# Four engine lists in a new order, and the query variance in one step per column block

## The chip, the cores and the metric

One core of one Trainium2 chip runs the whole model. The metric is the device time of one execution in microseconds; three runs of the kernel before gave 465.56, 465.67 and 467.3 us, median 465.67. Lower is better.

## What is computed

x is four sequences of 256 tokens, 128 wide. Two layers are applied, each an attention over a context and a feed-forward part, both behind a tanh gate; every part takes the layer norm of x.

```python
x = x + tanh(g_xattn[0]) * autocorrelation_attention(ln(x), ctx)   # FFTs over the sequence, top 5 delays
x = x + tanh(g_ffn[0])   * product_key_experts(ln(x))
x = x + tanh(g_xattn[1]) * rotary_attention(ln(x), ctx)            # 16 heads of 8
x = x + tanh(g_ffn[1])   * routed_experts(ln(x))                   # 8 experts, 336 wide
# product_key_experts, its head:
q = x @ w_q                                       # 128 -> 2048
q = (q - mean(q)) * rsqrt(var(q) + 1e-5) * bn_gamma + bn_beta     # over all 1024 tokens
sim = q . keys                                    # 2 x 8 heads x 32 keys
sx, sy = top_k(sim[0], 8), top_k(sim[1], 8)       # then top 8 of the 64 sums: 64 experts a token
h = softmax(scores) * gelu(x . down_embed[i]);  out = sum(h * up_embed[i])
# routed_experts: for each expert e
out += score[e] * (silu(x @ gate_w[e].T) * (x @ up_w[e].T)) @ down_w[e].T
```

## The kernel before

The program is written for each engine by hand: TensorE (PE in the profile), VectorE (DVE), ScalarE (ACT), GpSimd (POOL) and SyncE (SP), with semaphores between them. Each engine takes its instructions strictly in the order in which they are written, so an instruction that waits holds all that stand behind it. The first 90 us (the first attention, the layer norm of all 1024 tokens, the head of the product-key part) have an order fixed in the code. From there on the work is cut into named steps, and the string ORDER (line 60) lists for each engine which step comes next; the function `steps` reads it. A word is the step's name, a digit for the sequence b (0 to 3), a point and a number k: `token1.4` is step `token`, sequence 1, piece 4; `norms10.0` is `norms1`, sequence 0; `turn_32.0` is `turn_3`, sequence 2.

The query variance (lines 898 to 905). The variance of each of the 2048 query columns comes from the covariance of the normed x, cov (128x128). TensorE forms cov times w_q for 16 blocks of 128 columns, three blocks to a PSUM bank (six banks, the last with one block). VectorE copies the means, multiplies the bank by w_qT (L904), waits for that, and sums each block (L905). From the 16 x 128 variances come scaled keys keyS (L914) and, with 16 small matmuls, the matrix M; ScalarE copies M, and then `similar` t multiplies the tokens of tile t by M. `down_all` n forms one half of x times the embedding table (PE), which `gelu` n takes (ACT). EARLY says how many of them stand ahead of M's matmuls: with EARLY = 4, three on TensorE's list, n = 0 to 2, and three gelus on ScalarE's.

The steps that this text speaks of, in the order in which one sequence passes them:

- `best`, `where`, `pair` (DVE: L929, L936, L942 to L945), with `cands`, `gap`, `look_a` (POOL): the top 8 of each group and of the sums. `weight` (DVE, L978 to L992) turns them into expert numbers and weights; it waits for `look_a`, `gap` (POOL) and `soft` (ACT). `number` (POOL) splits the expert numbers and waits for both `weight` steps of its sequence. `onehots` (PE, then ACT) transposes them, `groups` (DVE, L1009 to L1027) makes the one-hot Y.
- `place` (DVE, L1035) makes a one-hot X for 16 tokens, `token` (PE, ps<-Y,Xb) multiplies it by Y, `half` (ACT, L611) copies, `weigh` (DVE, L1047 and L1052) forms HD. `mix` (PE, 16 matmuls of ps<-sb_upl,HDb) gives the part's output.
- `norms1` (DVE L1060 to L1068, then POOL L439 to L446, then ACT L627) adds it to x and normalises; `turn_2`, `query` (PE), `rope` (DVE L786 to L791), `turn_q` (PE, then ACT), four `by_query` (PE, ps<-KTb,Sb) and `max` (DVE L1097), `neg_max`, four `score` (PE, ps<-Sb,KTb), `prob` (ACT L651), `value` (PE, ps<-probs,V), `keep` (ACT), `out_turn`, `attend`, `project`: the second attention.
- `norms3` (DVE, POOL, ACT), `turn_3` (PE L1515), `route1` and `route2` (PE, ACT, DVE), `rank` (DVE); 21 `gate` (PE, ps<-...,sb_guT, into two banks by turns), 21 `silu` (ACT L694), 21 `times` (POOL L433 for sequences 0 and 1, DVE L1167 for 2 and 3), 8 `down` (PE, ps<-dnb,Sb) and `gather` (DVE L1155, L1157), `moe_out`. `addb` (POOL L459) adds a bias to x.

TensorE's bank 2 and bank 3 are each used by many steps in turn; `claim` makes each wait until the one before has been taken out, so a `down` waits for the `gather` of the last `down` or the `keep` of the last `value`. On ScalarE, `table` (L564) loads the function table where exp, gelu and silu follow each other.

The lines of VectorE that the second part of the change touches:

```python
v.tensor_copy(var[:, 2, c0:c0 + m], cw[:, :, D])
link(v.tensor_tensor(w, cw[:, :, 0:D], ld["w_qT"][:, c0:c0 + m, :], ALU.mult))
i = v.tensor_reduce(var[:, 3, c0:c0 + m], w, AX, ALU.add)
i.then_inc(sem("cw_used"), 1)
```

## Time and profile before

| what | value |
|---|---|
| median of three runs | 465.67 us |
| the profiled execution, own time | 464.96 us |
| its span, first to last instruction | 462.8 us |
| TensorE / VectorE / ScalarE / GpSimd busy | 381.2 / 331.8 / 193.8 / 108.9 us |
| mean granted clock of TensorE | 0.856 |

Busy time is a share of the whole span and mixes stages with different limits. TensorE's records overlap the pipeline, so its busy time is no measure of its peak; idle time ahead of a row, in square brackets, names who released it. The granted clock is given in tenths of full speed: 5 is 1.2 GHz, 10 (printed 9 or 1.00) is 2.4 GHz.

### The profile page before, as it was taken

The page shows a single profiled execution, that of the slowest core. Times are in us where ns is not written, and L with a number is a line of the kernel's source. Part 1 is how long each engine was busy: PE and PEld are TensorE (multiplying, and loading weights), DVE is VectorE, ACT ScalarE, POOL GpSimd, SP SyncE. Part 2 cuts the span into 40 slices and gives each one's busy share as a digit, 9 for nine tenths or more (in the row PEclk, how much of TensorE's full clock was granted, in tenths as well). Part 3 has the DMA queues.
Part 4 walks back from the last instruction along what each step waited for, and adds up shares of the span by engine and source line. Part 5 has one row for each costly group of instructions (what it writes and reads, how often), then busy time and mean ns, then how long its engine had stood idle before and what let it go on. Part 6 is the DMA issues. An engine that isn't in the chain of part 4 may idle for free.

```text
span 462.8 us, 7976 instructions
## 1 busy us (share of the span) xinstructions
PE 381.2 (82%) x2812; PEld 293.8 (63%) x2812; DVE 331.8 (72%) x1235; ACT 193.8 (42%) x393; POOL 108.9 (24%) x221
## 2 busy tenths in 40 slices
...
DVE  6996575999999999999998385866416543344533
...
PEclk9989897985565555766589999999999999999999
...
GB/s 220 336 220 0 1 1 2 1 157 2 1 1 0 2 0 1 1 1 1 1 0 2 1 2 1 1 3 12 1 1 1 0 13 2 1 0 1 11 1 11
DMA packets 5773, 11.80 MB, mean 25 GB/s; under 512 B 2021, under 2 KB 4326, under 8 KB 5223
## 3 DMA queue, kind: packets, MB, share of 16 engines
...
q14 instruction: 17, 0.13, 0.1%
...
## 4 chain that ended last, share of the span: by engine, by line
PE 39%; DVE 9%; ACT 3%; issue 3%; POOL 1%; POOLq 0%; DVEq 0%; ACTq 0%
PE ps L1193 37%; DVE Y L1027 2%; DVE Xb L1035 1%; PE ps L1435 1%; DVE mx L1097 1%; ACT L564 1%; ACT Sb L694 1%; DVE sb_downT L1017 1%; DVE Sb L1167 1%; DVE xnb L1157 0%; DVE HDb L1052 0%; ACT probs L651 0%; POOL rs L441 0%; ACT xnb L627 0%; PE ps L1515 0%
## 5 line engine op out<-in xcount | busy, mean ns | idle before, releaser
L1193 PE MATMUL ps<-dnb,Sb 128*128 128x128 f32 x448 | 57.1, 279 | 3.9 <-DVE xnb L1157 1.5
L1193 PEld LDWEIGHTS ps<-dnb,Sb 128*128 128x128 f32 x448 | 53.2, 192 | 9.8 <-issue 7.1
L1193 PE MATMUL ps<-Y,Xb 128*128 128x32 f16 x512 | 39.9, 250 | 18.8 <-DVE Xb L1035 13.2
L1193 PEld LDWEIGHTS ps<-Y,Xb 128*128 128x128 f16 x512 | 36.9, 164 | 27.3 <-DVE Xb L1035 18.3
L694 ACT ACTIVATE Sb<-ps 128x256 f32<-128x256 f32 x84 | 31.3, 380 | 41.5 <-PE ps L1193 41.4
L471 ACT ACTIVATE Sb<-ps 128x256 f32<-128x256 f32 (+2 forms) x54 | 26.6, 494 | 43.7 <-PE ps L1193 32.3
L1193 PE MATMUL ps<-ctxTb,sb_guT 128*128 128x256 f32 x168 | 44.0, 396 | 0.8 <-DVE Sb L1167 0.7
L1035 DVE TENSOR_TENSOR Xb<-sb_downT,iox 128x2048 f16<-128x2048 f16 x32 | 40.4, 1274 | 4.6 <-PE ps L1193 4.4
L1193 PE MATMUL ps<-Xb,sb_guT 128*128 128x256 f32 x168 | 43.1, 398 | 0.3
L1097 DVE TENSOR_REDUCE mx<-ps 128x8 f32<-128x2048 f32 x16 | 36.6, 2289 | 5.0 <-PE ps L1193 4.7
L1157 DVE SCALAR_TENSOR_TENSOR xnb<-ps,score,xnb 128x128 f32<-128x128 f32 x56 | 17.0, 345 | 31.4 <-PE ps L1193 31.3
L564 ACT ACT_TABLE_LOAD x29 | 37.2, 1283 | 0.5
L651 ACT ACTIVATE probs<-ps 128x1024 f32<-128x1024 f32 x32 | 31.4, 1018 | 10.9 <-PE ps L1193 10.8
L1193 PEld LDWEIGHTS ps<-Xb,sb_guT 128*128 128x128 f32 x168 | 30.9, 197 | 7.1 <-DVE Sb L1167 1.7
L1167 DVE TENSOR_TENSOR Sb<-Sb,ps 128x256 f32<-128x256 f32 x42 | 17.1, 419 | 25.0 <-ACT Sb L694 24.9
L1193 PEld LDWEIGHTS ps<-ctxTb,sb_guT 128*128 128x128 f32 x168 | 30.1, 194 | 7.8 <-DVE Sb L1167 2.1
L433 POOL TENSOR_TENSOR Sb<-Sb 128x256 f32<-128x256 f32 x28 | 24.3, 879 | 33.6 <-ACT Sb L694 33.4
L1193 PE MATMUL ps<-KTb,Sb 32*128 32x256 f32 x256 | 24.0, 501 | 9.1 <-DVE mx L1097 4.9
L1193 PE MATMUL ps<-sb_upl,HDb 128*128 128x128 f32 x128 | 20.2, 332 | 5.4 <-DVE HDb L1052 5.4
L1193 PEld LDWEIGHTS ps<-sb_upl,HDb 128*128 128x128 f32 x128 | 19.5, 244 | 7.3 <-DVE HDb L1052 7.3
L1193 PEld LDWEIGHTS ps<-KTb,Sb 32*128 32x128 f32 x256 | 14.5, 235 | 14.7 <-DVE mx L1097 6.3
L382 POOL TENSOR_SCALAR tixf<-tix 128x64 f32<-128x64 uint32 x8 | 4.0, 503 | 80.3 <-DVE tix L936 80.3
...
## 6 DMA issues: line engine op xcount, KB each, us to landing
...
```

The source lines that it names most:

```text
L433: g.tensor_tensor(av[:, m % 6, :], av[:, m % 6, :], up[m % 3], ALU.mult).then_inc(sem("av_ready"), 1)
L471: act.activation(dst, src, ACT.Copy, scale=scale).then_inc(sem(s), 1)
L564: act.activation(sm[:, 63:64], tg[:, 0:1], func).then_inc(sem("table_ready"), 1)
L651: act.activation(probs[:, g % 2, 2 * half:2 * half + 2, :], ps[:, 4 + 2 * half:6 + 2 * half, :], ACT.Exp, scale=float(1.0 / np.sqrt(DK))). ...
L694: act.activation(av[:, m % 6, :], ps[:, m % 2, 0:256], ACT.Silu).then_inc(sem("gate_ready"), 1)
L1017: link(v.tensor_tensor(elS[:, :, :], elT[:, 0, :].unsqueeze(1).broadcast_to([P, EH, P]), ld["io16"][:, :].unsqueeze(2).broadcast_to([P, EH ...
L1027: i = v.tensor_tensor(Y[r, q, k, :, :], Yq[r, :, :], whl[r, k, :].unsqueeze(1).broadcast_to([64, EH, P]), ALU.mult)
L1035: v.tensor_tensor(X[:, c % 2, :, :].rearrange("p (c e) t -> p c e t", c=EH), elS[:, :, c * TC:c * TC + TC].unsqueeze(2).broadcast_to([P, E ...
L1097: v.tensor_reduce(mx[:, :, 4 * g:4 * g + 4].rearrange("p t r -> p r t"), ps[:, 4:8, :].rearrange("p r (t k) -> p r t k", t=2), AX, ALU.max)\
L1157: i = v.scalar_tensor_tensor(macc[:, t, :], y, w, macc[:, t, :], ALU.mult, ALU.add)
L1167: v.tensor_tensor(av[:, m % 6, :], av[:, m % 6, :], ps[:, m % 2, 256:512], ALU.mult).then_inc(sem("av_ready"), 1)
L1193: return pe.matmul(o, l, r, start=start, stop=stop)
```

## The change

First, ORDER is replaced: each engine's list holds the same steps as before (244 for TensorE, 210 for ScalarE, 217 for VectorE, 76 for GpSimd), in another order. Second, the variance: instead of one multiply and one sum for a bank of three blocks, with a wait between them, there is one `scalar_tensor_tensor` for each block, which multiplies twice (once by 1.0) and gives the sum of its products in an accumulated output. Third, EARLY goes from 4 to 2: one `down_all` and one `gelu` stand ahead of M, the others of the first four behind the first four `similar`. The diff, the lists cut to the lines that the text speaks of:

```diff
     "pe": """
-onehots0.0 token0.0 token0.1 token0.2 token0.3 token0.4 token0.5 token0.6 token0.7 mix0.0 turn_20.0 query0.0 turn_q0.0
-onehots1.0 by_query0.0 by_query0.1 token1.0 by_query0.2 token1.1 by_query0.3 token1.2 neg_max0.0 token1.3 score0.0
-token1.4 score0.1 value0.0 token1.5 score0.2 token1.6 value0.1 score0.3 token1.7 value0.2 mix1.0 value0.3 onehots2.0
-out_turn0.0 turn_21.0 query1.0 attend0.0 project0.0 turn_q1.0 token2.0 by_query1.0 turn_30.0 token2.1 gate0.0
...
-gate0.6 route20.0 neg_max1.0 token2.5 score1.0 token2.6 gate0.7 score1.1 value1.0 token2.7 score1.2 value1.1 mix2.0
-score1.3 value1.2 onehots3.0 down0.0 down0.1 gate0.8 gate0.9 turn_22.0 gate0.10 query2.0 gate0.11 gate0.12 value1.3
-turn_q2.0 down0.2 by_query2.0 gate0.13 out_turn1.0 gate0.14 by_query2.1 down0.3 token3.0 attend1.0 by_query2.2
...
-score3.0 down1.7 gate2.2 route22.0 score3.1 gate2.3 value3.0 value3.1 score3.2 down2.0 gate2.4 gate2.5 score3.3
-value3.2 gate2.6 gate2.7 down2.1 gate2.8 down2.2 gate2.9 value3.3 gate2.10 out_turn3.0 gate2.11 gate2.12 down2.3
-gate2.13 attend3.0 gate2.14 project3.0 gate2.15 gate2.16 down2.4 gate2.17 down2.5 gate2.18 gate2.19 turn_33.0 gate2.20
-down2.6 gate3.0 gate3.1 route13.0 gate3.2 route23.0 down2.7 gate3.3 gate3.4 gate3.5 down3.0 gate3.6 gate3.7 down3.1
...
+onehots0.0 token0.0 token0.1 token0.2 token0.3 token0.4 token0.5 token0.6 token0.7 mix0.0 onehots1.0 turn_20.0
+query0.0 turn_q0.0 token1.0 token1.1 by_query0.0 token1.2 token1.3 by_query0.1 token1.4 by_query0.2 token1.5
+by_query0.3 token1.6 neg_max0.0 token1.7 score0.0 mix1.0 score0.1 value0.0 onehots2.0 score0.2 value0.1 score0.3
+value0.2 turn_21.0 value0.3 query1.0 out_turn0.0 turn_q1.0 attend0.0 project0.0 by_query1.0 token2.0 turn_30.0
+token2.1 gate0.0 by_query1.1 gate0.1 token2.2 gate0.2 by_query1.2 gate0.3 token2.3 gate0.4 by_query1.3 route10.0
+token2.4 gate0.5 neg_max1.0 route20.0 token2.5 score1.0 gate0.6 gate0.7 token2.6 value1.0 score1.1 down0.0 token2.7
+score1.2 value1.1 mix2.0 down0.1 gate0.8 onehots3.0 gate0.9 value1.2 gate0.10 down0.2 gate0.11 score1.3 turn_22.0
+gate0.12 query2.0 down0.3 token3.0 turn_q2.0 value1.3 token3.1 by_query2.0 gate0.13 out_turn1.0 gate0.14 by_query2.1
...
+project2.0 score3.0 gate1.16 down1.4 gate1.17 down1.5 gate1.18 turn_32.0 gate1.19 gate1.20 route12.0 gate2.0 score3.1
+down1.6 gate2.1 route22.0 score3.2 value3.0 gate2.2 down1.7 gate2.3 value3.1 score3.3 value3.2 down2.0 gate2.4
+value3.3 gate2.5 out_turn3.0 gate2.6 gate2.7 down2.1 gate2.8 attend3.0 gate2.9 project3.0 gate2.10 gate2.11 down2.2
+gate2.12 down2.3 gate2.13 gate2.14 turn_33.0 gate2.15 down2.4 gate2.16 down2.5 gate2.17 gate2.18 route13.0 gate2.19
+route23.0 gate2.20 down2.6 gate3.0 gate3.1 down2.7 gate3.2 gate3.3 gate3.4 gate3.5 down3.0 gate3.6 down3.1 gate3.7
...
     "act": """
...
-keep0.0 half1.5 soft2.1 prob0.4 prob0.5 keep0.1 half1.6 prob0.6 prob0.7 half1.7 keep0.2 keep0.3 onehots2.0 norms1_b1.0
-soft3.0 soft3.1 turn_21.0 attend0.0 turn_q1.0 half2.0 norms3_b0.0 turn_30.0 half2.1 silu0.0 half2.2 silu0.1 silu0.2
-silu0.3 half2.3 silu0.4 half2.4 route10.0 silu0.5 neg_max1.0 half2.5 prob1.0 half2.6 prob1.1 route20.0 prob1.2 prob1.3
-half2.7 keep1.0 prob1.4 prob1.5 keep1.1 prob1.6 keep1.2 prob1.7 onehots3.0 norms1_b2.0 silu0.6 silu0.7 silu0.8 silu0.9
...
-turn_33.0 silu2.20 silu3.0 route13.0 silu3.1 silu3.2 route23.0 silu3.3 silu3.4 silu3.5 silu3.6 silu3.7 silu3.8 silu3.9
...
+turn_20.0 soft2.0 half1.0 turn_q0.0 half1.1 half1.2 half1.3 half1.4 half1.5 soft2.1 half1.6 neg_max0.0 half1.7 prob0.0
+prob0.1 prob0.2 prob0.3 onehots2.0 keep0.0 prob0.4 prob0.5 soft3.0 norms1_b1.0 keep0.1 prob0.6 prob0.7 keep0.2
+turn_21.0 keep0.3 attend0.0 turn_q1.0 half2.0 norms3_b0.0 turn_30.0 half2.1 silu0.0 silu0.1 half2.2 silu0.2 silu0.3
+half2.3 silu0.4 route10.0 half2.4 silu0.5 neg_max1.0 route20.0 half2.5 prob1.0 prob1.1 keep1.0 half2.6 prob1.2 soft3.1
+prob1.3 half2.7 prob1.4 silu0.6 keep1.1 silu0.7 prob1.5 silu0.8 onehots3.0 norms1_b2.0 keep1.2 silu0.9 silu0.10
+silu0.11 turn_22.0 prob1.6 prob1.7 half3.0 turn_q2.0 keep1.3 silu0.12 silu0.13 half3.1 silu0.14 silu0.15 half3.2
...
+silu2.9 silu2.10 silu2.11 norms3_b3.0 silu2.12 silu2.13 turn_33.0 silu2.14 silu2.15 silu2.16 silu2.17 silu2.18
+route13.0 silu2.19 silu2.20 route23.0 silu3.0 silu3.1 silu3.2 silu3.3 silu3.4 silu3.5 silu3.6 silu3.7 silu3.8 silu3.9
...
     "dve": """
...
-weigh0.2 weigh0.3 place0.5 weigh0.4 place0.6 weigh0.5 place0.7 weigh0.6 where1.0 weigh0.7 pair1.0 where1.1 weight1.0
-norms10.0 best2.0 pair1.1 where2.0 weight1.1 rope0.0 best2.1 pair2.0 groups1.0 max0.0 place1.0 place1.1 max0.1
-weigh1.0 place1.2 max0.2 weigh1.1 place1.3 max0.3 neg_max0.0 weigh1.2 place1.4 weight2.0 weigh1.3 place1.5 where2.1
-weigh1.4 pair2.1 place1.6 weigh1.5 place1.7 weight2.1 weigh1.6 best3.0 best3.1 weigh1.7 where3.0 where3.1 pair3.0
-norms11.0 pair3.1 groups2.0 place2.0 attend0.0 place2.1 weight3.0 rope1.0 norms30.0 weight3.1 weigh2.0 max1.0 weigh2.1
-place2.2 place2.3 max1.1 weigh2.2 place2.4 max1.2 weigh2.3 place2.5 weigh2.4 max1.3 neg_max1.0 route20.0 place2.6
-weigh2.5 place2.7 weigh2.6 rank0.0 weigh2.7 norms12.0 gather0.0 groups3.0 place3.0 place3.1 gather0.1 rope2.0
...
+weight1.0 norms10.0 weight1.1 best2.0 where2.0 groups1.0 best2.1 place1.0 pair2.0 rope0.0 place1.1 weight2.0 weigh1.0
+place1.2 place1.3 weigh1.1 where2.1 weigh1.2 max0.0 place1.4 place1.5 weigh1.3 max0.1 weigh1.4 pair2.1 max0.2 place1.6
+weigh1.5 max0.3 weigh1.6 neg_max0.0 place1.7 weight2.1 weigh1.7 best3.0 where3.0 best3.1 pair3.0 norms11.0 where3.1
+groups2.0 weight3.0 rope1.0 attend0.0 place2.0 place2.1 norms30.0 pair3.1 weigh2.0 max1.0 weigh2.1 place2.2 place2.3
+max1.1 weigh2.2 place2.4 max1.2 weigh2.3 max1.3 neg_max1.0 weigh2.4 place2.5 route20.0 place2.6 weigh2.5 rank0.0
+place2.7 weigh2.6 gather0.0 weigh2.7 weight3.1 norms12.0 gather0.1 groups3.0 place3.0 gather0.2 rope2.0 gather0.3
...
     "pool": """
-look_a0.1 cands1.0 cands1.1 look_a1.0 gap1.0 look_a1.1 norms10.0 cands2.0 gap1.1 look_a2.0 number1.0 cands2.1 gap2.0
-addb0.0 look_a2.1 gap2.1 number2.0 cands3.0 cands3.1 look_a3.0 look_a3.1 norms11.0 gap3.0 addb1.0 gap3.1 norms30.0
-number3.0 times0.0 times0.1 times0.2 times0.3 times0.4 times0.5 norms12.0 addb2.0 times0.6 times0.7 times0.8 times0.9
...
+look_a0.1 cands1.0 gap1.0 cands1.1 look_a1.0 gap1.1 look_a1.1 norms10.0 number1.0 cands2.0 look_a2.0 cands2.1 gap2.0
+gap2.1 look_a2.1 cands3.0 look_a3.0 number2.0 addb0.0 norms11.0 gap3.0 look_a3.1 cands3.1 norms30.0 gap3.1 times0.0
+times0.1 times0.2 times0.3 times0.4 times0.5 number3.0 times0.6 norms12.0 times0.7 times0.8 times0.9 times0.10
...
         G_BANK = [4 + n % 4 for n in range(2 * EH)]
-        EARLY = 4
+        EARLY = 2
         WARM = 3
         DIRECT = (2, 3)
...
             copy(M[:, :], ps[:, 7, :], "M_ready")
             similar(2)
             similar(3)
-            gelu(EARLY - 1)
-            for n in range(EARLY, EH):
+            for n in range(EARLY - 1, 4):
+                gelu(n)
+            for n in range(4, EH):
                 similar(n)
                 gelu(n)
             soft(0, 0)
...
                 cw = ps[:, bank, 0:m * (D + 1)].rearrange("p (c d) -> p c d", d=D + 1)
                 w = tmp[:, c0 * D:(c0 + m) * D].rearrange("p (c d) -> p c d", d=D)
                 v.tensor_copy(var[:, 2, c0:c0 + m], cw[:, :, D])
-                link(v.tensor_tensor(w, cw[:, :, 0:D], ld["w_qT"][:, c0:c0 + m, :], ALU.mult))
-                i = v.tensor_reduce(var[:, 3, c0:c0 + m], w, AX, ALU.add)
+                for c in range(m):
+                    i = v.scalar_tensor_tensor(w[:, c, :], cw[:, c, 0:D], 1.0, ld["w_qT"][:, c0 + c, :], ALU.mult, ALU.mult,
+                                               accum_out=var[:, 3, c0 + c:c0 + c + 1])
                 i.then_inc(sem("cw_used"), 1)
             v.wait_ge(sem("cw_used"), len(CW_BANK))
             link(v.tensor_tensor(var[:, 2, :], var[:, 2, :], var[:, 2, :], ALU.mult))
...
             for t in range(4):
                 shifted(t)
             pe.wait_ge(sem("xn1T_ready"), 1)
-            for n in range(3):
+            for n in range(EARLY - 1):
                 down_all(n)
             for c in range(16):
                 if c % 8 == 0:
...
             pe.wait_ge(sem("xcT_ready"), 1)
             for t in range(4):
                 similar(t)
-            down_all(3)
+            for n in range(EARLY - 1, 4):
+                down_all(n)
             for t in range(4, NT):
                 shifted(t)
                 similar(t)
```

## Rows read from the trace of the kernel before

**Rows 1.** Page, part 2: VectorE busy tenths and granted clock in 40 slices of the span.

```profile
DVE  6996575999999999999998385866416543344533
...
PEclk9989897985565555766589999999999999999999
```

**Rows 2.** Windows: stretch in us, then busy us (instructions) per engine, PEclk, DMA.

```profile
80.00:220.00 140.00, 84.99 (x614) 59.68 (x612) 136.26 (x695) 36.23 (x72) 47.55 (x112) 0.64 0.04 14
...
247.00:283.00 36.00, 32.27 (x321) 25.01 (x320) 23.68 (x53) 21.77 (x45) 9.97 (x16) 1.00 0.00 1
...
366.00:392.00 26.00, 24.48 (x213) 17.94 (x212) 8.67 (x34) 22.18 (x41) 3.29 (x6) 1.00 0.02 7
...
420.00:432.00 12.00, 10.35 (x51) 7.93 (x50) 6.76 (x27) 8.49 (x16) 0.00 (x0) 0.86 0.01 1
```

**Rows 3.** Timeline of PE, 57 to 73 us: start, duration, operation [idle before, releaser].

```profile
57.54 3.74 PE L1193 MATMUL ps<-Gb,simb 128*128 128x129 f32 x32
...
64.55 2.74 PE L1193 MATMUL ps<-dnb,sb_downT 128*128 128x512 f32 x6
...
67.27 3.76 PE L1193 MATMUL ps<-Gb,simb 128*128 128x32 f32 x32
```

**Rows 4.** Timeline of DVE, 52 to 65 us.

```profile
52.70 1.37 DVE L894 TENSOR_SCALAR xnb<-sb_x,mv,rs 128x128 f32<-128x128 f32 x5
...
58.48 0.16 DVE L903 COPY var<-ps 128x3 f32<-128x3 f32 x1 [4.42 <-PE ps L1193]
...
58.56 0.55 DVE L904 TENSOR_TENSOR Gb<-ps,simb 128x384 f32<-128x384 f32 x1
...
59.61 0.15 DVE L903 COPY var<-ps 128x3 f32<-128x3 f32 x1
...
64.79 0.17 DVE L908 TENSOR_TENSOR var<-var 128x16 f32<-128x16 f32 x1
```

**Rows 5.** Timeline of DVE, 99 to 264 us.

```profile
99.23 3.06 DVE L929 MAX8 top<-simb 128x8 f32<-128x32 f32 x32
...
221.22 0.40 DVE L786 TENSOR_TENSOR Sb<-ps,cs 128x256 f32<-128x256 f32 x1
...
223.63 0.83 DVE L978 TENSOR_TENSOR hot<-pkf,iox 128x1280 f16<-128x1280 f16 x1
...
227.52 0.41 DVE L1047 TENSOR_TENSOR Xb<-Xb,ps 128x256 f32<-128x256 f32 x1
...
263.00 0.48 DVE L1060 SCALAR_TENSOR_TENSOR sb_x<-ps,tg,sb_x 128x256 f32<-128x256 f32 x1 [4.27 <-PE ps L1193]
```

**Rows 6.** Timeline of POOL, 207 to 215 us.

```profile
207.15 0.22 POOL L439 TENSOR_SCALAR rs<-mv 128x2 f32<-128x2 f32 x1 [1.50 <-DVE mv L1068]
...
211.79 0.62 POOL L446 TENSOR_TENSOR nb<-rs 128x2 f32<-128x2 f32 x1
...
213.47 1.01 POOL L459 TENSOR_TENSOR sb_x<-sb_x,sb_bo 128x256 f32<-128x256 f32 x1
```

**Rows 7.** Timeline of PE, 198 to 283 us.

```profile
198.82 1.43 PE L1193 MATMUL ps<-sb_upl,HDb 128*128 128x128 f32 x5 [1.47 <-DVE HDb L1052]
...
216.43 0.77 PE L1193 MATMUL ps<-sb_Wq,ctxTb 128*128 128x128 f32 x2 [2.36 <-ACT ctxTb L471]
...
225.63 2.09 PE L1193 MATMUL ps<-KTb,Sb 32*128 32x256 f32 x16
...
228.75 0.69 PE L1515 MATMUL ps<-sb_ident,xnb 128*128 128x128 f32 x2 [1.04 <-ACT xnb L627]
...
238.30 1.15 PE L1193 MATMUL ps<-KTb,Sb 32*128 32x256 f32 x16
```

**Rows 8.** Timeline of PE, 425 to 431 us.

```profile
425.98 4.43 PE L1193 MATMUL ps<-Xb,sb_guT 128*128 128x256 f32 x12
```

**Rows 9.** Page, part 5: groups of ScalarE: busy us, mean ns; idle before.

```profile
L564 ACT ACT_TABLE_LOAD x29 | 37.2, 1283 | 0.5
...
L651 ACT ACTIVATE probs<-ps 128x1024 f32<-128x1024 f32 x32 | 31.4, 1018 | 10.9 <-PE ps L1193 10.8
```

More of the change, by code:

```diff
@@ L82 @@
+gate2.12 down2.3 gate2.13 gate2.14 turn_33.0 gate2.15 down2.4 gate2.16 down2.5 gate2.17 gate2.18 route13.0 gate2.19
+route23.0 gate2.20 down2.6 gate3.0 gate3.1 down2.7 gate3.2 gate3.3 gate3.4 gate3.5 down3.0 gate3.6 down3.1 gate3.7
+gate3.8 gate3.9 gate3.10 down3.2 gate3.11 down3.3 gate3.12 gate3.13 gate3.14 gate3.15 down3.4 gate3.16 gate3.17
+gate3.18 gate3.19 down3.5 gate3.20 down3.6 down3.7
 """,
     "act": """
-onehots0.0 half0.0 half0.1 half0.2 half0.3 half0.4 half0.5 half0.6 half0.7 soft1.0 norms1_b0.0 turn_20.0 soft1.1
@@ L95 @@
[L95 to L98 removed]
+onehots0.0 half0.0 half0.1 half0.2 half0.3 half0.4 half0.5 half0.6 half0.7 soft1.0 soft1.1 onehots1.0 norms1_b0.0
@@ L112 @@
-weigh3.5 moe_out0.0 weigh3.6 weigh3.7 rank1.0 norms13.0 gather1.0 gather1.1 rope3.0 gather1.2 gather1.3 max3.0
-attend2.0 max3.1 gather1.4 max3.2 norms32.0 max3.3 gather1.5 neg_max3.0 gather1.6 times2.0 times2.1 gather1.7
-moe_out1.0 route22.0 rank2.0 times2.2 times2.3 gather2.0 times2.4 times2.5 times2.6 times2.7 gather2.1 gather2.2
-times2.8 times2.9 times2.10 attend3.0 times2.11 times2.12 gather2.3 times2.13 times2.14 norms33.0 times2.15 gather2.4
-times2.16 times2.17 gather2.5 times2.18 times2.19 times2.20 gather2.6 times3.0 route23.0 times3.1 times3.2 rank3.0
```

55 lines of the change are left out of this document (27 added, 28 removed).

## The prediction

> **What bounds the kernel now.** I read the busy slices first, then busy time by windows, then each engine's timeline, laid step by step against ORDER (the number of instructions of each step is known from the code, so every row has its step). Two stages follow each other. From 80 to 220 us VectorE is busy 136.3 of 140 us, while TensorE has 85 busy us and, mostly, half the clock [rows 1, 2]; its list sets the pace. From the start of `turn_30.0` at 228.75 [rows 7] the gates exist, and TensorE has work to the end: between 247 and 283 us it idles 3.7 us, between 366 and 392 1.5, between 420 and 432 1.65 [rows 2]. What TensorE has to do from `turn_30.0` on is, but for the order, the same set of steps in both lists. So the time is the start of `turn_30.0`, plus that work, plus the waits and half-clock stretches in it. An order that only shuffles the second stage can win those waits and no more.
>
> **The head: variance and EARLY.** The block runs on VectorE from 58.48 to 64.79, 6.3 us, 1.13 a bank of three blocks [rows 4]. The new form has six copies, 0.08 each to the next instruction, and 16 products of 128x128; five plain 128x128 instructions take 1.37, so 0.27 each [rows 4]: 0.5 + 4.3 = 4.8 us, 1.5 less. No row shows an accumulated output. It costs nothing at the least; at the most I take another small instruction, 0.08 as the copy has, which is 16 x 0.08 = 1.3 us and leaves a gain of 0.2. I take the middle, **-0.9 us**, range 0.2 to 1.5. In VectorE's page of the Trainium skill ("VectorE: DVE Perf Modes", section "Two Vector instructions with no wait between them") such an operation counts as two instructions, the main one and an accumulator read; no run here shows it yet. By that rule the gain would be 0.2, without it 1.5.
> TensorE must be there as soon: M's matmuls start at 67.27, straight behind three `down_all` (64.55, 2.74 for three) [rows 3]. With EARLY = 4 no gain on VectorE could pass; with 2 it is free at 64.55 + 0.91 = 65.5, room for 1.8. The two products and gelus that are moved stand behind the first four `similar`, ahead of tiles that VectorE needs much later. They cost nothing while ScalarE's `soft` 0 comes in time for `weight0.0`; if not, the 0.9 is lost there.
>
> **VectorE up to `weigh1.7`.** In the old order the last piece of sequence 1 is weighed just ahead of 198.82, where `mix1.0` starts [rows 7]. The new list has the same steps ahead of it but `best3.0` and `best3.1`, 2 x 1.53 [rows 5]: -3.0 us. New waits are possible in two places. `onehots1.0` stands ahead of `turn_20.0` on both TensorE and ScalarE and waits for `number1.0`, which waits for `weight1.1`: `groups1.0` may come 0.6 late. And `weight2.0` stands close behind `gap2.0`: 0.3. The four `max0` now alternate with `place` and `weigh`, each long enough to cover a half-clock `by_query` of 2.1. Sum **-2.1**, `weigh1.7` ends at about 195.8. Between -3 and -1.
>
> **From `weigh1.7` to `turn_30.0`: the step that costs.** Old: 198.8 to 228.75, 30 us, VectorE full. By VectorE's work alone the new `rope1.0` could start some 20 us behind `weigh1.7` (old 22.4 [rows 5], less `pair3.1`, two `place` and `attend0.0`, plus two `best`). But the whole of sequence 0's attention has slipped to this place, and the normalising of sequence 1 stands in one line with it. GpSimd: `number2.0`, `addb0.0` (1.0), `norms11.0` (207.15 to 212.4, 5.3 beside `groups2.0`), `gap3.0` (1.1) [rows 6]. ScalarE: `soft3.0` waits for that `gap3.0`, and `norms1_b1.0` and `keep0.1` stand behind it, then two `prob` of 1.0 [rows 9]. TensorE: `value0.2` waits for `keep0.1`, `value0.3` for the last `prob`, and `query1.0` stands behind it, 3 us at half clock (216.43 to 219.4) [rows 7]. Adding up: `norms11.0` done on VectorE +9, on GpSimd +15, `gap3.0` +16, `norms1_b1.0` and `keep0.1` +17.8, both `prob` +19.8, `value0.3` +21.7, `query1.0` +25. VectorE stands 4 us in front of `rope1.0`, and `attend0.0`, `project0.0` and `norms30.0` follow the same thread: `turn_30.0` +36 with all of it at half clock, +33 with full clock for half of it, since TensorE is denser here than before. I take 34.4, **+4.4**; ends 30 and 36.5. `weight3.1` (3.9 us, 223.63 to 227.52) leaves this stretch for the hole of 4.27 us ahead of `norms12.0` at 263.00 [rows 5], so VectorE isn't late afterwards.
> **Clock.** At half clock a `by_query` takes 2.09, at full 1.15 [rows 7]. Old, the slices up to 231 show half [rows 1], with `turn_30.0`'s first gate and `by_query1.1` in them. With less idling ahead, half of these 1.9 us come back: **-0.9**, 0 to 1.9.
>
> **Stage two.** *Sequence 1's values, 247 to 283.* Old waits 3.7 us: `down0.1` for a `gather`, `value1.3` behind them. New, `down0.0` is ahead of `token2.7`, `gather0.0` ahead of `weigh2.7`, and four gates and `down` stand between `score1.3` and `value1.3`. Followed through with the old durations, TensorE waits about 0.4: **-3.3**, range -3.7 to 0. *Sequence 3's attention*, 366 to 392: `score3.0` and 3.1 go ahead; of 1.5 waiting us 0.7 stay (`score3.3` behind two `prob` and a table load): **-0.8**. *`route13.0`, `route23.0`*: they now stand ahead of sequence 2's last gates. Old, 1.65 of idling in 420 to 432 [rows 2], and then three gates at 4.43 where full clock would give some 3.0 [rows 8]: 3.1; new, `route23.0` waits 0.8 for the gelu table and gate3.2 0.7 behind `rank3.0`: **-1.5**. *What I can't follow:* the new ScalarE list changes its function 28 times, the old 26, so the loads go from 29 to 31, each 1.28 and a 0.20 start [rows 9], 3.0 us in all, and other waits arise between 283 and 420, where the old order lost only some 0.6 in 83 us. I put **+1.5** for both, 0 to 4.
>
> **Sum.** -0.9 - 2.1 + 4.4 - 0.9 - 3.3 - 0.8 - 1.5 + 1.5 = -3.6 us. On the profiled execution: 464.96 - 3.6 = 461.4 (462.8 of span and 2.2 around it). The median of the runs stands 0.7 above the profiled one: 465.67 - 3.6 = **462.1 us**.
>
> **Rivals.**
> *A. The thread doesn't bind.* GpSimd's `norms11.0` isn't slowed as in its 5.3 us before, the clock is full, `rope1.0` starts on VectorE's own time, `turn_30.0` keeps the 30 us: 462.1 - 4.4 = 457.7. For it: TensorE's dense list there. Against: `gap3.0` sits in front of three ScalarE steps whatever the clock.
> *B. Nothing is won in stage two.* The waits only move, since each `down` still needs the last `gather`, and table loads eat the rest; all but 1.5 of the 5.6 recovered us is given back: 462.1 + 4.1 = 466.2, no change. For it: 283 to 420 shows that the old order was already close.
> *C. Slower.* The thread from `gap3.0` by `keep0.1` to `query1.0` runs at half clock, `turn_30.0` comes +36.5 behind `weigh1.7`, at 232.3, and TensorE starts its gates at half clock as before: +2.1 and +0.9 on the forecast; with stage two winning only 1.6 of 5.6, 462.1 + 7.0 = 469.1. It decides from a `turn_30.0` later than 231 us together with over 3 us of waits between 247 and 283. For it: each link of the thread is in the lists. Against: VectorE enters it 3 us earlier.
>
> **How the numbers follow.** Forecast 0.49, A 0.15, B 0.20, C 0.16. Its own parts' bounds give the forecast 458.5 to 465.5. A measurement of this kernel tells 0.5%, 2.3 us, from no change: below 463.3 is faster, above 468.0 slower. Of the forecast's 0.49 some 0.40 lie below 463.3 and the rest in between; A is faster with 0.15; B gives 0.04 to faster, 0.14 to the middle and 0.02 to slower; C 0.13 slower, 0.03 between. Faster 0.59, same 0.26, slower 0.15. The range takes in A and most of C: 457.0 to 468.5.
>
> **What would show it.** The head: `similar` 0 done on VectorE about 0.9 earlier, the block shorter than 6.3 us. `weigh1.7` ending near 195.8. An idle time of about 4 us of VectorE in front of `rope1.0`, and `turn_30.0` near 230. Less than 1 us of TensorE idle in the 36 us after `neg_max1.0`. 31 loads. I am wrong if `rope1.0` doesn't wait (A), or if TensorE's waits behind `turn_30.0` in the three stretches of [rows 2] add up to more than the old 6.9 us (B, C).

## The result, and the profile after

The changed kernel takes 461.47 us (median of 20 runs, 458.27 to 465.73); the kernel before, run beside it, 465.62 us. The ratio is 0.9914, 95% interval 0.9893 to 0.9935: 4.0 us faster. Forecast were 462.1 us and, against the median before, -3.6 us. The profiled execution took 461.36 us with a span of 459.3. The run of 465.73 us is in a slower state of the chip, and the ratio leaves it out.

The page's part 2 of the kernel after, answering [rows 1]; VectorE is at 9 for 11 slices in a row from the eighth on, where it was 14:

```profile
DVE  7896658999999999997888687963547225435443
PEclk9989899975575555596598999999999999998999
```

Busy time by windows of the kernel after, answering [rows 2] (columns: window, its length, then busy us of PE, PEld, DVE, ACT, POOL, the granted clock, DMA share, GB/s):

```profile
80.00:220.00 140.00, 82.16 (x622) 59.61 (x624) 132.34 (x636) 35.98 (x71) 41.62 (x103) 0.64 0.04 14
247.00:283.00 36.00, 34.27 (x334) 27.67 (x335) 27.15 (x59) 24.21 (x46) 13.43 (x21) 0.98 0.01 2
366.00:392.00 26.00, 24.68 (x220) 18.37 (x219) 9.28 (x34) 18.71 (x34) 2.59 (x4) 1.00 0.03 7
420.00:432.00 12.00, 10.43 (x66) 9.00 (x65) 7.00 (x25) 2.58 (x7) 0.00 (x0) 1.00 0.04 11
```

TensorE idles 1.73, 1.32 and 1.57 us in the three later windows, 4.6 together where it was 6.9. That looks like the forecast; the waits over the whole stage, further down, show that it isn't.

TensorE's timeline around M, answering [rows 3] (columns: start, us, engine and line, tiles, count of records, in brackets the idle time ahead and who released it; each f32 matmul of 512 columns has two records). One `down_all` stands ahead of M's matmuls (64.19), M starts at 65.04 instead of 67.27, and the four `similar` follow at 69.38, the three others of the first four `down_all` at 72.92:

```profile
64.19 1.02 PE L1195 MATMUL ps<-dnb,sb_downT 128*128 128x512 f32 x2
65.04 3.65 PE L1195 MATMUL ps<-Gb,simb 128*128 128x32 f32 x32
69.38 3.70 PE L1195 MATMUL ps<-dnb,HDb 128*128 128x512 f32 x8 [0.69 <-ACT dnb L471]
72.92 2.74 PE L1195 MATMUL ps<-dnb,sb_downT 128*128 128x512 f32 x6
```

VectorE's timeline of the new variance, answering [rows 4]: the first bank and the end of the block. A product starts every 0.21 us; the accumulator read is a record of its own, and the next product starts at the same time as it:

```profile
58.12 0.16 DVE L904 COPY var<-ps 128x3 f32<-128x3 f32 x1 [4.42 <-PE ps L1195]
58.19 0.28 DVE L906 SCALAR_TENSOR_TENSOR Gb<-ps,simb 128x128 f32<-128x128 f32 x1
58.40 0.09 DVE L906 DVE_READ_ACCUMULATOR Gb<-ps,simb 128x1 f32 x1
58.40 0.29 DVE L906 SCALAR_TENSOR_TENSOR Gb<-ps,simb 128x128 f32<-128x128 f32 x1
...
62.02 0.17 DVE L910 TENSOR_TENSOR var<-var 128x16 f32<-128x16 f32 x1
```

VectorE ahead of and behind `rope1.0`, answering [rows 5], and, in the second fence, TensorE's `value0.2`, `query1.0` (four rows from 211.17, the first shown) and `turn_30.0`, answering [rows 7]:

```profile
212.99 0.39 DVE L787 TENSOR_TENSOR Sb<-ps,cs 128x256 f32<-128x256 f32 x1 [1.84 <-issue]
...
215.49 0.36 DVE L1110 RECIPROCAL rcp<-ps 128x32 f32<-128x32 f32 x1 [1.26 <-PE ps L1195]
...
219.52 0.48 DVE L1062 SCALAR_TENSOR_TENSOR sb_x<-ps,tg,sb_x 128x256 f32<-128x256 f32 x1 [0.94 <-PE ps L1195]
```

```profile
207.33 1.93 PE L1195 MATMUL ps<-probs,V 128*32 128x256 f32 x16 [2.20 <-ACT Sb L471]
...
211.17 0.49 PE L1195 MATMUL ps<-sb_Wq,ctxTb 128*128 128x128 f32 x2
...
224.55 0.69 PE L1518 MATMUL ps<-sb_ident,xnb 128*128 128x128 f32 x2 [1.86 <-ACT xnb L628]
```

The thread of the forecast (the chain of waits from GpSimd's `gap3.0` by ScalarE's `keep0.1` to TensorE's `query1.0`) is there: GpSimd took 4.7 us for `norms11.0` (200.33 to 205.06, against 5.3 in [rows 6]) and then `gap3.0`, which released ScalarE's `soft3.0` at 205.90; `norms1_b1.0` and `keep0.1` at 206.83 follow, and `value0.2` waited for that. ScalarE's timeline, and the page's group of table loads, answering [rows 9]:

```profile
205.90 0.26 ACT L583 ACTIVATE ex_<-dd 128x64 f32<-128x64 f32 x1 [1.96 <-POOL dd L413]
206.06 0.86 ACT L628 ACTIVATE xnb<-sb_x,nb,rs 128x128 f32<-128x128 f32 x2
206.83 0.36 ACT L471 ACTIVATE Sb<-ps 128x256 f32<-128x256 f32 x1
```

```profile
L564 ACT ACT_TABLE_LOAD x31 | 39.8, 1283 | 0.6
```

### The profile page after: what moved, and what is told of

The parts are those of the page before. It is cut to its first block, busy times and chain, and to the rows that moved or that the text cites. A ratio compares the mean times of both kernels' runs of the same rounds, so it can differ in the third digit from the quotient of the medians.

```text
span 459.3 us, 8002 instructions
## 1 busy us (share of the span) xinstructions
PE 376.1 (82%) x2812; PEld 292.1 (64%) x2812; DVE 328.6 (72%) x1255; ACT 196.2 (43%) x397; POOL 105.5 (23%) x221
## 4 chain that ended last, share of the span: by engine, by line
PE 42%; DVE 23%; POOL 6%; issue 4%; ACT 4%; DVEq 0%; POOLq 0%; ACTq 0%
PE ps L1195 40%; DVE Xb L1037 4%; DVE mx L1099 3%; DVE tix L938 2%; DVE HDb L1054 2%; DVE top L931 1%; PE ps L1438 1%; DVE hot L986 1%; DVE hot L984 1%; ACT L564 1%; DVE pk L947 1%; DVE hot L980 1%; POOL rs L441 1%; ACT probs L652 1%; DVE Xb L1049 1%
## 5 line engine op out<-in xcount | busy, mean ns | idle before, releaser
L1195 PE MATMUL ps<-dnb,Sb 128*128 128x128 f32 x448 | 58.1, 283 | 3.8 <-ACT Sb L471 2.3
L1195 PEld LDWEIGHTS ps<-dnb,Sb 128*128 128x128 f32 x448 | 55.2, 197 | 9.2 <-issue 5.1
L695 ACT ACTIVATE Sb<-ps 128x256 f32<-128x256 f32 x84 | 31.8, 381 | 41.2 <-PE ps L1195 41.2
L1195 PE MATMUL ps<-ctxTb,sb_guT 128*128 128x256 f32 x168 | 45.9, 403 | 0.0
L1037 DVE TENSOR_TENSOR Xb<-sb_downT,iox 128x2048 f16<-128x2048 f16 x32 | 39.0, 1233 | 0.2
L652 ACT ACTIVATE probs<-ps 128x1024 f32<-128x1024 f32 x32 | 31.4, 1018 | 12.9 <-PE ps L1195 12.8
L1195 PEld LDWEIGHTS ps<-Xb,sb_guT 128*128 128x128 f32 x168 | 29.3, 190 | 9.9 <-DVE Sb L1169 3.6
L433 POOL TENSOR_TENSOR Sb<-Sb 128x256 f32<-128x256 f32 x28 | 22.9, 821 | 55.2 <-ACT Sb L695 55.2
L1195 PE MATMUL ps<-Sb,KTb 32*128 32x256 f32 x256 | 20.2, 433 | 3.4 <-ACT probs L652 2.6
L612 ACT ACTIVATE Xb<-ps 128x256 f32<-128x256 f32 x16 | 6.1, 380 | 37.9 <-PE ps L1195 37.9
```

The source lines that it names most:

```text
L433: g.tensor_tensor(av[:, m % 6, :], av[:, m % 6, :], up[m % 3], ALU.mult).then_inc(sem("av_ready"), 1)
L652: act.activation(probs[:, g % 2, 2 * half:2 * half + 2, :], ps[:, 4 + 2 * half:6 + 2 * half, :], ACT.Exp, scale=float(1.0 / np.sqrt(DK))). ...
L695: act.activation(av[:, m % 6, :], ps[:, m % 2, 0:256], ACT.Silu).then_inc(sem("gate_ready"), 1)
L1037: v.tensor_tensor(X[:, c % 2, :, :].rearrange("p (c e) t -> p c e t", c=EH), elS[:, :, c * TC:c * TC + TC].unsqueeze(2).broadcast_to([P, E ...
L1195: return pe.matmul(o, l, r, start=start, stop=stop)
```

## How the runs are compared

Laid against ORDER, each trace gives two lengths: from the start of `weight0.0` (the first step of VectorE's list) to `turn_30.0`, and from there to the end of TensorE's last `down3.7`. "First part" below is the lists up to and with `turn_30.0` (TensorE, ScalarE) and `norms30.0` (VectorE, GpSimd); "second part" is all behind. All ratios are to the kernel before, run on the same chip. The lengths are of one execution each, the ratios of all.

| kernel | ratio, 95% interval | weight0.0 | to turn_30.0 | to the end |
|---|---|---|---|---|
| before | 1 | 90.0 | 138.7 | 230.4 |
| variance alone | 1.0002, 0.9979 to 1.0024 | 89.7 | 138.4 | 229.9 |
| EARLY = 2 alone | 1.001, 0.9986 to 1.0035 | 92.7 | 138.3 | 232.3 |
| head (both) | 0.9938, 0.9915 to 0.9961 | 86.6 | 138.4 | 232.4 |
| lists alone | 0.9991, 0.9966 to 1.0016 | 89.8 | 141.2 | 229.7 |
| head, new first part | 1.0059, 1.0034 to 1.0085 | 87.1 | 138.6 | 236.3 |
| head, new second part | 0.9866, 0.9838 to 0.9894 | 87.1 | 137.2 | 227.6 |
| the whole change | 0.9914, 0.9893 to 0.9935 | 85.9 | 138.7 | 231.1 |

In the two executions of before and after, TensorE's `turn_30.0` starts 4.2 us earlier (228.75 and 224.55), and the stage behind it is 0.7 us longer. By the ratios three quarters of the gain are the head's: the lists as a whole add 0.24% to it (0.9938 to 0.9914, overlapping intervals) and 0.09% to the kernel before. Neither is clear of noise. What follows on the halves of the lists is on two effects that nearly cancel.

## Experiments on the head

**The head alone.** The changed kernel with the old lists.

```diff
-        EARLY = 4
+        EARLY = 2
-                link(v.tensor_tensor(w, cw[:, :, 0:D], ld["w_qT"][:, c0:c0 + m, :], ALU.mult))
-                i = v.tensor_reduce(var[:, 3, c0:c0 + m], w, AX, ALU.add)
+                for c in range(m):
+                    i = v.scalar_tensor_tensor(... accum_out=var[:, 3, c0 + c:c0 + c + 1])
```

> The head alone: variance in one step per block and EARLY = 2, the four lists in the old order. Theory (the head gives nearly all): the profile after shows weight0.0 of sequence 0 starting 4.1 us earlier, of which 2.4 us is the variance and 2.4 us the four similar at full clock instead of half. In the old order VectorE sets the pace from there to turn_30.0, so the 4.1 us should pass to turn_30.0 (near 224.6) and to the end: about 461.5 us, ratio 0.991. Rival (the prediction's own sizes): the head gives 0.9 us, 464.7 us, ratio 0.998, and the rest of the gain is the lists'. Second rival: similar runs at full clock only by chance of the profiled execution; then weight0.0 starts 1.9 us earlier and the time is 463.7.

462.26 us, ratio 0.9938: -0.62% of 464.8 is -2.9 us, three times the prediction's 0.9, over a quarter less than the 4.1 that I expected. `weight0.0` came at 86.6, but in this execution the variance block itself began 1.1 us earlier than before (57.42 and 58.48). TensorE's timeline shows the first four `similar` at neither of the two lengths that I had seen (6.69 before, 3.70 in the whole change) but between:

```profile
64.34 3.65 PE L1195 MATMUL ps<-Gb,simb 128*128 128x32 f32 x32
68.68 5.40 PE L1195 MATMUL ps<-dnb,HDb 128*128 128x512 f32 x8 [0.69 <-ACT dnb L471]
```

The granted clock was 0.96 over 58 to 70 us and 0.50 between 70 and 72. Among the ten traces of kernels with both edits, the experiments below included, the same instructions took 5.40 us in seven and 3.70 in three; in the three with the old EARLY they took 6.69, 6.56 and 6.13, and with EARLY = 2 alone 5.48. The stretch at clock 0.50 that slows them lasted 6.8 us with the old EARLY, 3.4 in the seven, and was absent in the three. So the 2.4 us of the variance block are the change's; of `similar`, 0.7 to 1.3 us came back in every execution with both edits, and another 1.7 in three of ten. Counted from the start of the variance block, `weight0.0` came after 31.5 us before and 31.6 and 31.8 in the two others with the old EARLY, after 28.6 to 29.3 in the seven and 27.8 in the three: the head is worth 2.2 to 2.9 us as a rule and 3.8 at best, which fits the 2.9 of the ratio. Why the clock falls for less long is not shown.

**Its two edits one by one**, both with the old lists.

```diff
         EARLY = 4
+                for c in range(m):
+                    i = v.scalar_tensor_tensor(...)
```

> The variance in one step alone; EARLY stays 4 and the lists stay old. Theory (both edits are needed): VectorE is done 2.4 us sooner (block 3.9 instead of 6.3 us), but M's matmuls still stand behind three down_all and start near 67.0 as before; weight0.0 stays at about 90, and the time is that of before, 465 us, ratio 1.000. Rival: the variance alone carries the head's gain, since it also frees VectorE for what follows; then weight0.0 starts at 86 to 88 and the ratio is 0.994 as with the whole head.

```diff
-        EARLY = 4
+        EARLY = 2
```

> EARLY = 2 alone; the old variance and the old lists. Theory: TensorE is free at 65.0 but keyS comes only at 67, so M starts no earlier and idles about 1.5 us; weight0.0 at 89 to 90, ratio 1.000. Rival: the gain of the head is that similar runs at full clock when the down_all stand behind it; then similar takes 3.7 to 5.4 us instead of 6.7 and weight0.0 starts 1.3 to 2.4 us earlier, ratio 0.996.

Neither gives anything: 1.0002 and 1.001. TensorE's timeline of the variance alone: M still starts behind three `down_all`, at 66.58:

```profile
64.01 2.74 PE L1195 MATMUL ps<-dnb,sb_downT 128*128 128x512 f32 x6
66.58 4.18 PE L1195 MATMUL ps<-Gb,simb 128*128 128x32 f32 x32
```

and of EARLY = 2 alone: TensorE is free early and waits 1.70 us for the scaled keys, after which even M ran mostly at clock 0.50 (6.53 us; 3.65 at full clock in the whole change):

```profile
64.46 1.02 PE L1194 MATMUL ps<-dnb,sb_downT 128*128 128x512 f32 x2
67.18 6.53 PE L1194 MATMUL ps<-Gb,simb 128*128 128x32 f32 x32 [1.70 <-DVE Gb L915]
```

M needs VectorE's scaled keys, begun at 66.79 before and at 64.02 in the whole change, and TensorE, free at 67.3 [rows 3] and 65.0: a gain on one alone is nothing, on both M starts 2.2 us earlier.

## Experiments on the lists

**The lists alone**: the old variance and EARLY = 4 with the new ORDER.

```diff
-ORDER = { ... the old lists ... }
+ORDER = { ... the new lists ... }
```

> The new lists alone, with the old variance and EARLY = 4. Theory (the head gives nearly all): the lists give 3.7 us before the end of weigh1.7 and take 3.6 back before turn_30.0, and stage two wins nothing: 465.6 us, ratio 1.000. Rival (the prediction): the lists alone give 2.7 us, 462.9 us, ratio 0.994, with under 1 us of TensorE idling between by_query2.0's stretch of 36 us.

465.43 us, 0.9991: nothing that can be measured. The comparison of the traces before and after (up to `weigh1.7` -3.7, from there to `turn_30.0` +3.6) had led me to "the lists are worth nothing". For the lists as a whole that holds; for their halves it doesn't, as the next two show.

**Each half of the lists with the new head.** A list is the new one up to the cut and the old one's remaining steps behind it, or the other way.

```diff
 first part (to turn_30.0, norms30.0):   -old  +new
 second part:                             old
```

> New head, new lists up to turn_30.0 (TensorE, ScalarE) and norms30.0 (VectorE, GpSimd), behind that the old order. Theory: the first part of the new lists is worth 0, so it comes out with the head alone, 461.5 us. Rival (the prediction's sizes): the first part costs 2.3 us without the second's gain of 4.1, 463.8 us with the measured head.

```diff
 first part (to turn_30.0, norms30.0):    old
 second part:                            -old  +new
```

> New head, old lists up to turn_30.0 and norms30.0, behind that the new order. Theory: the second part wins nothing, 461.5 to 462 us. Rival (the prediction): the new second part gives 4.1 us on top of the head, 457.4 us, with turn_30.0 at 224.6 and TensorE idle under 1 us in the stretch of sequence 1's values.

1.0059 and 0.9866. The theory (both halves are worth nothing) falls; the prediction's signs hold. On the head's 0.9938 the second part gives 0.72%, 3.4 us; the first part then takes 0.48%, 2.2 us (from 0.9866 to 0.9914). In the other order the first costs 1.2%, 5.6 us, and the second gives 1.45%, 6.7 us: the size of a half hangs on the other half. In part that comes from how the lists were cut. New first and old second part put `pair3.1` and `weight3.1` ahead of `weigh2.0` on VectorE, with a wait of 2.32 us for GpSimd between them, and TensorE's `token2.1` waits for `weigh2.0`, 4.2 us that no other kernel has:

```profile
230.62 1.25 PE L1195 MATMUL ps<-Y,Xb 128*128 128x32 f16 x16 [4.22 <-DVE Xb L1049]
```

Busy time from `turn_30.0` to the end shows where this lies (five kernels, the same columns as above). Before, and the head alone:

```profile
228.75:459.20 230.45, 221.46 (x1825) 179.94 (x1825) 129.16 (x286) 125.08 (x261) 50.93 (x88) 0.98 0.01 3
```

```profile
225.00:457.40 232.40, 223.62 (x1825) 181.19 (x1825) 129.31 (x286) 125.44 (x261) 50.14 (x88) 0.97 0.01 3
```

The head with the new first part; with the new second part; the whole change:

```profile
225.70:462.00 236.30, 223.41 (x1825) 181.49 (x1825) 134.26 (x296) 125.35 (x262) 51.39 (x90) 0.96 0.01 3
```

```profile
224.30:451.90 227.60, 218.84 (x1829) 177.79 (x1825) 132.85 (x294) 127.42 (x265) 50.65 (x89) 0.99 0.01 3
```

```profile
224.60:455.70 231.10, 222.37 (x1825) 180.74 (x1825) 132.24 (x294) 127.68 (x266) 53.05 (x90) 0.97 0.01 3
```

Length less PE's busy time is what TensorE waits: 9.0, 8.8, 12.9, 8.8 and 8.7 us. But for the mixed list with its 4.2, the stage has the same waits, old or new. What differs is the busy time of the same 1825 matmuls (the count of 1829 takes in four that end behind the start), 218.8 to 223.6. By the clock records of these traces the granted clock was 0.50 for 9.4, 14.8, 18.5, 5.5 and 13.3 us of the stage. Over all profiled executions with the second part as it stands, the stage took 230.4, 232.4, 229.9 and 232.3 us with the old lists (and 236.3 in the mixed one) and 231.1, 229.7, 227.6, 227.4, 228.5, 226.6 and 229.2 with the new (the later ones from the runs below): means 231.3, without the mixed one, and 228.6. It is not only these traces: the granted clock over the whole program, averaged over each kernel's runs, was 0.853 to 0.856 in the kernels with the old second part and 0.859 to 0.870 in those with the new one and the new head; in the lists alone it was 0.855.

About half of it is one place. In all five traces with the old second part the clock is 0.50 for 3.4 us from 3.0 to 3.5 us behind the start of `route23.0`, where gates of 1.0 us each take 4.43 for three [rows 8]. With the new one, which runs `route23.0` ahead of sequence 2's last gates and waits 0.81 us there, eight of nine traces (that of the pulled gates, below, included) have no such stretch. The ninth is the whole change's: it has one at 415.4, ahead of the window from 420 to 432. The same `down2.6` in the whole change, and then in the kernel with the new second part alone:

```profile
415.35 3.65 PE L1195 MATMUL ps<-dnb,Sb 128*128 128x128 f32 x16
```

```profile
413.19 2.02 PE L1195 MATMUL ps<-dnb,Sb 128*128 128x128 f32 x16
```

A stretch of 3.4 us costs 1.7; by the counts (five of five, one of the seven whose stages are averaged above) that makes some 1.5 of the 2.7 us between the means, an estimate. No run moved `route13.0` and `route23.0` alone.

**The thread by `gap3.0` loosened.** The whole change with one edit on ScalarE's list.

```diff
-prob0.4 prob0.5 soft3.0 norms1_b1.0 keep0.1 prob0.6 prob0.7 keep0.2
+prob0.4 prob0.5 keep0.1 prob0.6 prob0.7 soft3.0 norms1_b1.0 keep0.2
```

> The whole change with one edit on ScalarE's list: soft3.0 and norms1_b1.0 stand behind prob0.7 instead of ahead of keep0.1. Theory (the thread by gap3.0 binds VectorE in the first part): keep0.1 no longer waits for GpSimd, value0.2 loses its wait of 2.2 us, query1.0 starts 1.7 us earlier, VectorE's wait of 1.9 us ahead of rope1.0 goes, turn_30.0 comes 1.5 us earlier and the time is 460.0 us, ratio 0.988. Rival (the thread is not what costs; VectorE's late norms30.0 and TensorE's clock decide): turn_30.0 moves by less than 0.5 us, ratio 0.991 as the whole change.

459.15 us, ratio 0.987 (0.9849 to 0.989): 0.44% below the whole change. `value0.2` no longer waits and `rope1.0` starts straight behind `weight3.0`. VectorE's timeline there (the second row is `rope1.0`), then TensorE's `value0.2`:

```profile
213.85 0.27 DVE L994 TENSOR_TENSOR wts<-ex_,zz 128x64 f32<-128x64 f32 x1
214.03 0.40 DVE L787 TENSOR_TENSOR Sb<-ps,cs 128x256 f32<-128x256 f32 x1
```

```profile
207.59 1.07 PE L1195 MATMUL ps<-probs,V 128*32 128x256 f32 x16
```

From `weigh1.7` to `turn_30.0` it took 30.3 us instead of 33.6. That length is one execution's: the kernels of 0.981 and 0.9849 below have the same first part, or nearly, and took 34.2 and 33.8, with `query1.0` and `out_turn0.0` at half clock, and VectorE waited 1.45 and 0.77 us ahead of `rope1.0`. With the thread it waited 1.84 to 3.62 in four traces. `value0.2` waited in all four of these (2.20 to 2.76 us) and in none of the three with the edit. The direction is shown by the ratios of two pairs, whose intervals don't overlap; the size is 0.4 to 0.8% (0.8 from the two kernels below that differ in this edit alone, 0.981 and 0.9886).

**Gates pulled forward** into holes of TensorE, on the kernel with ratio 0.9866. ScalarE's and GpSimd's lists follow it: `attend0.0` ahead of `norms1_b1.0`, `turn_q1.0` and `half2.0` behind `silu0.1`, `soft3.1` behind `prob1.2`, `addb1.0` behind `times0.5`.

```diff
 TensorE
-turn_21.0 query1.0 attend0.0 project0.0 turn_q1.0 token2.0 by_query1.0 turn_30.0 token2.1 gate0.0 by_query1.1 gate0.1
+attend0.0 project0.0 turn_21.0 query1.0 turn_30.0 gate0.0 gate0.1 turn_q1.0 token2.0 by_query1.0 token2.1 by_query1.1
 VectorE
-groups2.0 place2.0 attend0.0 place2.1 weight3.0 rope1.0 norms30.0
+attend0.0 groups2.0 norms30.0 place2.0 place2.1 weight3.0 rope1.0
```

> The new head, the old lists up to turn_30.0 and the new ones behind it (which gave ratio 0.987), and sequence 0's end of attention pulled forward: attend0.0 of VectorE ahead of groups2.0, norms30.0 right behind it, attend0.0 and project0.0 of TensorE ahead of turn_21.0, and turn_30.0, gate0.0 and gate0.1 ahead of turn_q1.0, where TensorE idled 7.2 us ahead of turn_21.0 and query1.0. Theory (stage two is TensorE's work plus waits that no order removes, so only work moved into holes in front of it counts): turn_30.0 starts at 216 to 218, 4 to 5 us of TensorE's work leave the stage, by_query1.0 comes 0 to 1 us later, and the time falls by 3 us to 455.8 us, ratio 0.980. Rival (turn_30.0 and the gates are not the bound; VectorE's list to neg_max1.0 and the values of sequence 1 are): the gates come early, TensorE waits later by as much, and the ratio stays 0.986 to 0.988.

463.86 us, 0.9966 (0.9939 to 0.9992): a miss, 1% slower than without, worse than the rival. `turn_30.0` started at 218.2, as expected, but `turn_q1.0` stood behind it and two gates at half clock (3.75 us), `token2.0` behind that, and VectorE, whose list waits for its `half2.0`, had nothing to do:

```profile
226.21 0.42 DVE L1048 TENSOR_TENSOR Xb<-Xb,ps 128x256 f32<-128x256 f32 x1 [6.99 <-ACT Xb L611]
```

TensorE had waited 6.46 us ahead of `turn_30.0`. GpSimd took 5.2 us for `norms30.0`, twice as long as the 2.7 for `norms11.0` in the same execution; by that difference at most 2.5 of VectorE's 7 us are GpSimd's, and the rest is the order. GpSimd, the first three of each:

```profile
203.12 0.23 POOL L438 TENSOR_SCALAR rs<-mv 128x2 f32<-128x2 f32 x1 [1.49 <-DVE mv L1069]
203.41 0.23 POOL L439 TENSOR_SCALAR rs<-mv 128x2 f32<-128x2 f32 x1
203.72 0.73 POOL L440 TENSOR_TENSOR rs<-rs,nhalf 128x2 f32<-128x2 f32 x1
...
212.02 1.12 POOL L438 TENSOR_SCALAR rs<-mv 128x2 f32<-128x2 f32 x1 [5.08 <-DVE mv L1069]
213.20 1.06 POOL L439 TENSOR_SCALAR rs<-mv 128x2 f32<-128x2 f32 x1
214.35 1.14 POOL L440 TENSOR_TENSOR rs<-rs,nhalf 128x2 f32<-128x2 f32 x1
```

**The same pattern a sequence later.** On the kernel with the loosened thread.

```diff
-silu0.8 onehots3.0 norms1_b2.0 keep1.2
+silu0.8 onehots3.0 keep1.2 norms1_b2.0
```

> The whole change with two edits on ScalarE's list: the one that gave ratio 0.987 (soft3.0 and norms1_b1.0 behind prob0.7) and the same pattern a sequence later, keep1.2 ahead of norms1_b2.0 instead of behind it. Theory (what costs in these lists is a quick ScalarE step held behind one that waits for GpSimd): down0.2 of TensorE waited 1.75 us for keep1.2, which stood behind norms1_b2.0 and GpSimd's norms12.0; the wait goes, everything behind comes 1.7 us earlier, 457.5 us, ratio 0.9833. Rival (a removed wait of stage two comes back a step later, since the waits behind turn_30.0 summed to 8.7 to 9.0 us in either order): TensorE still idles 8.7 us behind turn_30.0, and the ratio stays 0.987.

457.54 us, 0.981 (0.9772 to 0.9848), the lowest of all. TensorE's timeline at `down0.2`, in the kernel with the loosened thread and in this one:

```profile
266.33 1.58 PE L1195 MATMUL ps<-dnb,Sb 128*128 128x128 f32 x12 [1.75 <-ACT Sb L471]
```

```profile
269.49 1.60 PE L1195 MATMUL ps<-dnb,Sb 128*128 128x128 f32 x12 [1.16 <-POOL Sb L433]
```

The wait shrank by 0.6 us and changed its releaser: now it is a `times` of GpSimd behind `norms12.0`. Over the stage TensorE waited 8.9 us, as the rival said (8.8 without the edit). Two more were to tell whether the lower median is the edit's: the whole change with this edit alone, and the kernel with ratio 0.9866 with it (the diff is the same).

> The whole change with keep1.2 ahead of norms1_b2.0 as its one edit. In the kernel with both ScalarE edits the waits of TensorE behind turn_30.0 summed to 8.9 us as without this one, since down0.2's wait of 1.75 us shrank to 1.16 (GpSimd's times behind norms12.0 released it then) and by_query1.3 waited 0.6; its median was 0.6% lower all the same, with overlapping intervals. If the wait only changed its releaser: ratio 0.991, as the whole change. If the edit is worth its 0.6%: 0.985, and by_query2.0 comes 0.6 us or more earlier behind turn_30.0 than the 56.3 us of the whole change.

> New head, old lists up to turn_30.0 and norms30.0, new ones behind (ratio 0.987 so far), and keep1.2 ahead of norms1_b2.0. If the wait only changed its releaser: ratio 0.987, TensorE idle 8.8 us behind turn_30.0. If the edit is worth 0.6%: 0.981, and the best of all versions.

0.9886 (0.9855 to 0.9917) against 0.9914, and 0.9878 (0.9847 to 0.9909) against 0.9866. `down0.2` waited 1.15 and 1.14 us, and over the stage TensorE waited 8.2 us (8.7 without the edit) and 9.1 (8.8): in one of the three pairs the 0.6 us did not come back. By the trace the edit is worth 0.6 us, 0.13%, at most; three pairs of runs (-0.6, -0.3, +0.1%) have overlapping intervals and can't tell more.

**Work into the wait ahead of `turn_30.0`**, on the kernel of 0.981. On ScalarE `half2.1` goes ahead of `turn_30.0` too.

```diff
-token2.0 turn_30.0 token2.1 gate0.0
+token2.0 token2.1 turn_30.0 gate0.0
```

> As the one with keep1.2, and token2.1 with its half2.1 ahead of turn_30.0, in the 1.86 us for which TensorE waits there. Theory: 1.2 us of work move into that wait, turn_30.0 starts where it was and the time is 456.3 us, ratio 0.981. Rival (VectorE or ScalarE set the pace to neg_max1.0): gate0.0 comes earlier but neg_max1.0 does not, ratio as without the edit.

459.61 us, 0.9849 (0.9809 to 0.9888), overlapping with 0.981: no gain. `token2.1` itself waited 1.02 us there and `gate0.0` 0.56, where `turn_30.0` alone had waited 1.87.

## Why the prediction was right, and where it was not

The total was right, in good part by luck. Adding the parts in the order head, second part, first part, the ratios give -2.9, -3.4 and +2.2 us, together -4.1. The prediction had -0.9, -5.0 (stage two -4.1, clock -0.9) and +2.3, together -3.6. The head was 2.0 us too small and the second part 1.6 too large, and the two misses cancel; the intervals make each part uncertain by some 1.5 us. In the other order the lists' parts are +5.6 and -6.7. What does not hang on the order is that the head gives 2.9 us and the lists together 1.1, where the prediction had 0.9 and 2.7.

Of its own signs, the block shorter than 6.3 us and the 31 table loads came. `weigh1.7` ended at 191.0, not near 195.8, and `turn_30.0` came at 224.6, not near 230: in the profiled execution the whole gain lies ahead of `turn_30.0` (-4.2 us against a forecast of about +1) and none behind it (+0.7 against -4.1). TensorE idled 1.9 us in the 36 us behind `neg_max1.0`, not under 1. The sign of being wrong, over 6.9 us of waits in the three stretches, did not show, since the waits had left these stretches and not the stage.

- *The head, -0.9.* Mis-sized: the block took 3.90 us, not 4.8 to 6.1, and the effect on `similar` and its clock, 0.7 us or more, had no term. The step that failed was the price of a product, 0.27, taken from [rows 4], and 0 to 0.08 on top for the accumulated output. The products start 0.21 apart with the accumulator read between them: it overlaps the next product. The Trainium skill ("VectorE: DVE Perf Modes", section "Two Vector instructions with no wait between them") counts two instructions, and the trace shows both records. The page gives no price; to read one into it was my step, and the second cost no time here. The bound of 1.5 for the gain was too low; the block became 2.4 us shorter. That the gain passes only with EARLY = 2 was right (1.0002 and 1.001 for each edit alone). Its room of 1.8 us was near: M started 2.2 us earlier, since the three `down_all` began at 64.55 and the one at 64.19.
- *VectorE up to `weigh1.7`, -2.1.* From `weight0.0` it took 108.8 us before and 105.1 after (104.8 and 105.0 in the two others with the new first part): -3.7. Of the waits I added, `weight2.0` had none and `groups1.0` 0.48 us.
- *From `weigh1.7` to `turn_30.0`, +4.4.* 33.6 us instead of 30.0, +3.6; with the lists alone 36.4, +6.4. The thread was right, shown by the run that loosens it. VectorE's 4 us ahead of `rope1.0` came as 1.84, 1.26 and 0.94 ahead of `rope1.0`, `attend0.0` and `norms30.0`: 4.0 in all. Rival A, that it doesn't bind, is out.
- *Clock, -0.9.* Not seen in the profiled execution: the first gate took 2.04 us and `by_query1.1` 2.09, as before, and the clock stayed at 0.50 until 6.5 us behind the start of `turn_30.0` (6.0 before).
- *Stage two, -4.1.* The mechanism failed, part of the size held. The waits that I followed did shrink where I looked, 6.9 to 4.6 us in three windows, but TensorE's waits over the stage stayed (9.0 and 8.7): `down0.2` now waits 1.7, `gate3.2` 1.4, `score2.1`, `score3.0` and `down0.6` 1.7 together. That is rival B's mechanism. What the new second part gives is TensorE at full clock more of the time. The means say -2.7, the ratios -3.4. About half of it is the one piece of clock that the sum did have, the three gates at 4.43 behind `route23.0`; there the waits grew (0.81 and 1.44 us against 0.97 and 0.68), and the half clock went in eight traces of nine. In the one profiled execution of the whole change, none of it is seen (231.1 us). Why the clock stays up there, and where the other half comes from, the runs don't settle.
- *31 table loads* came as said, with no cost that could be set apart.
- *Rival C* named the point from which it decides, `turn_30.0` later than 231 with over 3 us of waits between 247 and 283. The lists alone put it at 231.0 and came out at no change. Its thread at half clock is what their trace shows (36.4 us from `weigh1.7`, `query1.0` 2.97 us), but the 4.0 us that it gave back in stage two did not show there: that stage took 229.7 us, 0.7 less than before.
